# Sixteen attention heads written out with constants, and the weight pieces split in thirds at later steps

## What is computed

```python
scores = jnp.einsum('bhqd,bhkd->bhqk', q, k) * scale
scores = jnp.where(causal, scores, -jnp.inf)
attn = jax.nn.softmax(scores, axis=-1)
out = jnp.einsum('bhqk,bhkd->bhqd', attn, v)
...
geo = qp[..., :, None] * kp[..., None, :]
geo = jnp.where(causal, geo, -jnp.inf)
geo_attn = jax.nn.softmax(geo, axis=-1)
geo_out = jnp.einsum('bhqk,bhkd->bhqd', geo_attn, v)
out = out + head_scales[None, :, None, None] * jax.lax.stop_gradient(geo_out - out)
```

## Time and profile before

| | |
|---|---|
| median of 3 runs | 3029.93 us (3023.97 to 3037.75) |
| profiled execution | 3029.94 us, its span 3028.3 us |
| first and last exponential of the attention part (L801) | start at 318.0 and 1372.2 us |
| busy share of the span | PE 86%, DVE 73%, ACT 49%, POOL 18% |
| mean granted clock of TensorE | 0.932 |

### The profile page before, as it was taken

One profiled execution on the slowest core, in us unless ns is written; L12 is line 12 of the kernel. 1 busy time (PEld: TensorE's weight loads), 2 busy tenths in 40 slices (PEclk: granted clock), 3 DMA queues, 4 the chain that ended last, 5 costly groups with the idle time before them and its releaser, 6 DMA issues. The chain is left out here.

```text
span 3028.3 us, 47655 instructions
## 1 busy us (share of the span) xinstructions
PE 2605.3 (86%) x14040; PEld 1555.7 (51%) x14040; DVE 2209.3 (73%) x4456; ACT 1496.9 (49%) x2777; POOL 542.2 (18%) x356
## 2 busy tenths in 40 slices
PE   4995899899898899994399999948978999995998
PEld 2442333333333333332267777737866777774787
DVE  4876788788888788875678888825547888884665
ACT  0220455555555555561166666624425666664443
POOL 0110000000001000004433333300003333331000
PEclk7996899999999999997699999979999999998999
DMA  2334244433343344325310000030001000001111
GB/s 87 106 116 117 59 111 131 117 107 99 100 123 103 101 127 129 88 71 170 118 41 9 9 9 9 4 112 21 20 15 50 9 10 9 9 6 33 55 58 42
DMA packets 122758, 204.99 MB, mean 68 GB/s; under 512 B 21728, under 2 KB 69920, under 8 KB 119216
## 3 DMA queue, kind: packets, MB, share of 16 engines
q1 hardware_dynamic: 108912, 163.96, 19.5%
q0 software_dynamic: 7808, 21.79, 2.5%
q10 hardware_dynamic: 5920, 17.75, 1.6%
HBM read 125.30 MB, written 54.26 MB: 59 GB/s over the span
## 5 line engine op out<-in xcount | busy, mean ns | idle before, releaser
L801 ACT ACTIVATE probs<-st_ps 128x1024 f32<-128x1024 f32 (+3 forms) x640 | 547.2, 894 | 523.6 <-PE st_ps L733 247.8
L749 PE MATMUL o_ps<-probs,vx 128*33 128x512 f32 (+3 forms) x2560 | 557.4, 558 | 0.0
L850 DVE SCALAR_TENSOR_TENSOR st_ps<-geo_rows,kp_t 128x512 f32<-128x512 f32 (+3 forms) x640 | 445.6, 713 | 77.4 <-ACT probs L801 73.4
L831 DVE TENSOR_REDUCE chunk_max<-a_ps 128x1 f32<-128x512 f32 (+3 forms) x640 | 367.0, 605 | 90.5 <-PE a_ps L721 50.5
L719 PE MATMUL a_ps<-k,q 96*128 96x512 f32 (+3 forms) x640 | 273.7, 477 | 82.1 <-DVE chunk_max L831 66.5
L1224 PE MATMUL local_in_ps<-w_local,local_ht 128*128 128x512 f32 x1152 | 323.7, 418 | 10.3 <-ACT local_sq L1366 5.9
L1385 ACT ACTIVATE local_probs<-local_s_ps,local_bias,local_inv 128x256 f32<-128x256 f32 x512 | 282.6, 563 | 13.6 <-DVE local_bias L1480 13.5
L1660 PE MATMUL ff_ag_ps<-ff_ht_parts,w 128*128 128x512 f32 (+1 forms) x1056 | 260.0, 405 | 33.7 <-DVE ff_gate L1769 25.5
L719 PEld LDWEIGHTS a_ps<-k,q 96*128 96x128 f32 x640 | 123.9, 204 | 279.5 <-issue 154.7
L733 PE MATMUL st_ps<-q,k 98*128 98x512 f32 (+3 forms) x640 | 224.9, 415 | 38.3 <-ACT probs L801 31.9
L749 PEld LDWEIGHTS o_ps<-probs,vx 128*33 128x33 f32 x2560 | 125.6, 113 | 255.4 <-issue 202.3
(11 more groups left out here) (171 smaller groups left out, 3674.0 us busy)
## 6 DMA issues: line engine op xcount, KB each, us to landing
geo_rows<-geo SPq DMA_DIRECT2D x64, 512.0 KB, 7.2
q<-q_parts SPq DMA_DIRECT2D x48, 256.0 KB, 4.2
k<-k_parts SPq DMA_DIRECT2D x48, 256.0 KB, 6.4
piece_lo<-in_pieces POOLq DMA_DIRECT2D x15, 768.0 KB, 5.3
weight_parts<-piece_hi SPq DMA_DIRECT2D x15, 768.0 KB, 3.3
weight_parts<-piece_lo SPq DMA_DIRECT2D x15, 768.0 KB, 5.8
raw<-out_t SPq DMA_DIRECT2D x128, 64.0 KB
shares_in<-shares SPq DMA_DIRECT2D x64, 128.0 KB, 3.8
```

What stands on the lines that cost most here:

```text
L749: ins = pe.matmul(o_ps[kind * HALF:kind * HALF + VW, g % 2, off:GTOK], vx[s][:, j, :], probs[:, i % PSLOTS, kind, off:GTOK], start=j == 0, ...
L801: act.activation(probs[:, s % PSLOTS, :, off:GTOK], st_ps[:, s % 2, :, off:GTOK], ACT.Exp).then_inc(q["probs_ready"], 1)
L831: dve.reduce_max(chunk_max[:, it, c:c + 1], a_ps[:, s % 2, 0:n], AX.X).then_inc(q["a_used"], 1)
L850: ins = dve.scalar_tensor_tensor(out[:, off:GTOK], geo[:, 1, at], kp_t[:, j, ds(b, 1)].rearrange("p o -> p o"), geo[:, 0, at], ALU.add, AL ...
```

## The change

The loops of the attention part go: all five engines have heads 0 to 15 written out with constants. Each piece is split by thirds of 512 columns. ACT rounds one third behind each of the steps 28, 30 and 32, where it rounded the whole piece behind step 24. DVE subtracts one third behind each of the bursts 17, 18 and 19, where it subtracted the whole piece behind burst 16. SP waits for all three thirds before it stores.

```diff
-    FIRST_TURNS, LOOPED = 1, SETS * ((BH - 2) // SETS)
-    LAST_TURNS = range(FIRST_TURNS + LOOPED, BH)
+    THIRDS = [slice(n * PIECE // 3, (n + 1) * PIECE // 3) for n in range(3)]
+    HIGH_AFTER, LOW_AFTER = (28, 30, 32), BURSTS - 3
...
     def turns(eng, turn):
-        turn(0, 0, 0, False, True)
-        with eng.Fori(0, LOOPED // SETS) as n:
-            for i in range(SETS):
-                turn(SETS * n + (FIRST_TURNS + i), (FIRST_TURNS + i) % SETS, n + (FIRST_TURNS + i) // SETS, True, True)
-        for b in LAST_TURNS:
-            turn(b, b % SETS, b // SETS, True, b < BH - 1)
+        for b in range(BH):
+            turn(b, b % SETS, b // SETS, b > 0, b < BH - 1)
...
-                        sp.wait_ge(q[ready], k + 1 + START)
+                        sp.wait_ge(q[ready], 3 * k + 3 + START)
...
-                def piece_high(k):
+                def piece_high(k, third):
                     act.wait_ge(piece_in, 16 * k + 16)
-                    act.activation(piece_hi[:, :], piece_lo[:, :].bitcast(F32), ACT.Copy).then_inc(q["piece_hi"], 1)
+                    act.activation(piece_hi[:, third], piece_lo[:, third].bitcast(F32), ACT.Copy).then_inc(q["piece_hi"], 1)
...
-                        if more and s == 24:
-                            piece_high(b)
+                        if more and s in HIGH_AFTER:
+                            piece_high(b, THIRDS[HIGH_AFTER.index(s)])
...
-                turn(0, False, True)
-                with act.Fori(1, BH - 1) as b:
-                    turn(b, True, True)
-                turn(BH - 1, True, False)
+                for b in range(BH):
+                    turn(b, b > 0, b < BH - 1)
...
-                def piece_low(k):
-                    dve.wait_ge(q["piece_hi"], k + 1 + START)
-                    dve.tensor_tensor(piece_lo[:, :], piece_lo[:, :].bitcast(F32), piece_hi[:, :].bitcast(F32), ALU.subtract).then_inc(q["piece_lo"], 1)
+                def piece_low(k, n):
+                    third = THIRDS[n]
+                    dve.wait_ge(q["piece_hi"], 3 * k + n + 1 + START)
+                    dve.tensor_tensor(piece_lo[:, third], piece_lo[:, third].bitcast(F32), piece_hi[:, third].bitcast(F32), ALU.subtract).then_inc(q["piece_lo"], 1)
...
-                        if more and p == 16:
-                            piece_low(b)
+                        if more and p >= LOW_AFTER:
+                            piece_low(b, p - LOW_AFTER)
```

## The result

The changed kernel takes 2979.98 us (median of 4 runs, 2977.64 to 2983.97), beside 3030.88 us for the kernel before in the same comparison. The ratio is 0.9833 (95% interval 0.9808 to 0.9859): 50.9 us faster, where 59.4 us were forecast, and the time lies inside the forecast range of 2956 to 2994 us. The profiled execution has a span of 2980.4 us, 47.9 us shorter than that of before.

A forecast was written before the change was run, and what follows sets the result against it. It took a ring of PE, DVE and ACT over two score buffers to bound the attention part. Terms 22.8 + 21.0 + 27.3 - 7.5 - 4.2 = 59.4 us off 3029.9 gave 2970 us, range 2956 to 2994.

The forecast's parts named there:

- No jumps: Loop jumps behind heads 3, 6 and 9 vanish on DVE, PE, SP and POOL: 3 x 7.6 = 22.8 us go.
- Register instructions at nothing: Register instructions vanish on all engines; costed at nothing, since they hide behind the instruction ahead.
- No long copy behind step 24: DVE's 1.49 and PE's 1.39 us stall behind ACT's copy goes: 1.4 us a head, 15 heads, 21.0 us.
- No fall of the clock behind it, and two that come back: The 13 clock falls behind the copy's stall go, 27.3 us; two falls return, 4.2 us.
- Falls that come back: POOL's multiplication holds up DVE beside the thirds, so some heads fall again: two falls, 4.2 us back.
- Each time right behind this stall: Reading of the windows behind the 15 pieces: the clock fell 13 times, always directly after the step-24 copy's stall.
- Thirds: Split copies cost 0.3 us a head on ACT and 0.2 on DVE: 7.5 us back over 15 heads.
- The signs: Expected: no DVE issue idle of 4 us, stall gone, clock near 1.00, products 1.91 us, turn 62 to 63 us.
- The falls stay: Rival, 15%: the clock falls in each head anyway, at another short PE stall; 23.1 us lacking, 2993 us.
- The stall only moves: Rival, 9%: thirds delay steps 29, 31 and 33 by as much as the old stall; 3007 to 2995 us.
- Straight code is held up: Rival, 4%: written-out code waits for instruction fetches, 4.8 us a head, 72 us added; 3042.5 us.
- More than I count: Rival, 6%: thirds hidden, the old 1.75 us worth more, no fall left; 75 us gained, 2955 us.

The follow-up runs named there:

- the first run: The kernel before with all five engines written out with constants, the pieces left whole at their old places: 3009.22 us.
- the later versions: The changed kernel with DVE's thirds a burst earlier (2967.46 us), POOL's work on 8 columns (2960.36), or PE's third tile between the products (2951.26; with ACT's thirds early 2945.55).

## Why the prediction was right, and where its sizes were off

*No jumps.* Right. 22.8 us were forecast; the straight code alone gave 18.5 us, with an interval of 12 to 26 (0.0039 and 0.0085 of 3027.7). No "issue" wait of DVE or PE is left between heads. What the prediction didn't see is that the 7.6 us are not waiting alone: behind each jump the clock fell too, for 10.2 us, and the turn that it calls "no fall behind the piece" has such a fall in it (behind 786.6 us). These falls are not among its 13, so nothing is counted twice, and straight code took both away. That straight code is not held up is shown by the same run and by the count of instruction transfers, which went down.

*Register instructions at nothing.* Right as far as a run can tell: straight code gave no more than the jumps, and its turns without a fall are as long as before.

*No long copy behind step 24.* Right in its place: DVE's 1.49 and PE's 1.39 us are gone, 0.15 and 0.17 are left. Its size, 1.4 us a head, no run shows by itself. With thirds of 8 columns the turn is 1.1 us shorter than before, and that holds the stall, DVE's old 1.75 us and whatever the small thirds cost.

*No fall of the clock behind it, and two that come back.* The mechanism is right, and the number is wrong: this is the largest error. Six falls were left and not two, so 13 - 6 = 7 went, 7 x 2.1 = 14.7 us in place of 27.3 - 4.2 = 23.1. The step that failed is "Falls that come back". It looked only at POOL's hold on DVE, which gave two falls, heads 4 and 9, as it said. That they are just two is luck: the other versions with straight code, full thirds and POOL's full work had none to three there. The other four came from PE's wait of 0.89 us for DVE's maximum behind step 27. It stood in the trace of before, within a microsecond of the 1.39 us stall, so I had put every fall down to the longer one. "Each time right behind this stall" was a wrong reading: in heads 2, 3, 8, 12 and 13 the fall began behind the second wait, in head 2 at 496.5 us:

```profile
495.48 0.50 PE L719 MATMUL a_ps<-k,q 96*128 96x512 f32 x1 [0.89 <-DVE chunk_max L831]
...
496.50:499.90 3.40, 3.40 (x11) 0.84 (x6) 1.54 (x3) 0.00 (x0) 0.10 (x1) 0.50 1.00 262
```

The run with the third tile between the products took this wait away, and all falls behind step 27 went.

*Thirds.* The terms of the stall and the thirds were 21.0 - 7.5 = 13.5 us. Of the 44.7 us of the attention part, 22.8 for the jumps and 14.7 for the falls leave 7.2 us. The turns without a fall say less still: from 63.53 to 63.27 us, 0.26 us a head or 4 us. So the two terms together gave 4 to 7 us. If the stall was worth its 21.0, the thirds cost 13.8 us or more, at least 0.9 us a head where I had 0.5; how the shortfall splits between the two is not shown. One part of it is: 0.4 to 0.6 us a head at the change of heads, where the last third stands ahead of the first maxima. I had that place right and its share too small, as I set the old 1.75 us against it.

The differences, with the jumps held at 22.8: 8.4 us on the falls, 6.3 on the stall and the thirds, and 3.2 us the other way from the stages that weren't changed, together 11.5, which is what lies between 59.4 and the profiled 47.9. The 3.2 us are luck, and so are the 3 us between this profiled gain and the 50.9 of the medians.

*The signs.* Three were missed. The turn between two pieces is 63.27 us without a fall, where 62 to 63 was said, the products take 3.56 us behind a fall and not 1.91 in each head, and ACT's wait for PE in head 8, burst 16, is 0.39 us and not 0.1.

*Rivals.* "The falls stay" was half true (6 of 13). "The stall only moves" fell with the timeline. "Straight code is held up" fell with the first run. "More than I count" is not this change, but it was to be had: the later versions gained 60 to 84 us.

*What I would have told wrongly without the runs* is that splitting the copy on ACT matters. It doesn't: whole behind step 30 (2976.99 us), in early thirds (2977.18) and in late thirds (2979.98) it costs nearly the same, and the thirds early are at best 0.2 to 0.5 us a head better. Moving it off step 24 was nearly the whole gain there.

What stays open is why the same stall of 0.89 us is followed by a fall in some heads and not in others. In the run with POOL's work cut it was every second head, which speaks for a matter of when the stall comes and not of what it is; no run tells more.

## What to carry to other kernels

Look for a long instruction of side work between two steps of a ring of engines, and first try other places for it in that engine's queue; splitting it comes second. When a stall of PE is removed, list the next longest ones near it, since the clock may fall behind these too, and each fall costs more than the stall: 1.7 to 2.3 us here for 0.9 us of waiting. A jump back can cost at each pass, 7.6 us here for bodies of three heads, with the fall of the clock behind it, and most of it came with DVE's jump.

Compare versions by the turns without a fall and by the number of falls, and not by the time alone: here two versions differed by less than 1 us in time with two and with four falls.

## What the runs showed of the hardware

- Right behind a stall of PE of 0.89 us the granted clock went to 0.50 for 3.4 us, and the products behind it took 3.56 in place of 1.91 us. It did so in four of 15 like heads of the changed kernel and, with POOL's work cut, at every second head, and in none where the stall had been taken away.
- The price of a jump back is not alike: before, DVE waited 4.48 to 5.65 us for its next instruction and PE 1.47 to 1.84 us at the three jumps, and ACT with its loop of one head showed no "issue" wait. Behind each of the three the granted clock was 0.50 for 10.2 us.
- POOL's multiplication of 128x1024 (2.36 us) and addition (1.60 us), both on operands in SBUF, held four exponents of DVE for 6.50 us, where they take 0.76 us each alone. This agrees with the Trainium skill (SBUF — State Buffer, Who interferes with whom): a DVE instruction with two inputs in SBUF contends with a GpSimd instruction that reads there.
